# Values as high and low columns with sums on VectorE, and a conv with bf16 taps kept on chip

## The reference

```python
def _L0_cond_ref(x, mask, Wq, Wo):
    xt = jnp.transpose(x, (0, 2, 1))
    q = xt @ Wq.T
    qh = q.reshape(B, T, NH, dk).transpose(0, 2, 1, 3)
    scores = scale * jnp.einsum('bhqd,bhkd->bhqk', qh, qh)
    logits = (scores * cmask + (1.0 - cmask) * NEG) * rmask
    attn = jax.nn.softmax(logits, axis=-1)
    ctx = jnp.einsum('bhqk,bhkd->bhqd', attn, qh)
    out = ctx.transpose(0, 2, 1, 3).reshape(B, T, D) @ Wo.T
    return jnp.transpose(out, (0, 2, 1))

def _L1_cond_ref(x, w, b):
    y = jax.lax.conv_general_dilated(x, w, window_strides=(1,), padding=[(K - 1, 0)], feature_group_count=D, ...)
    return y + b

x = x + _L0_cond_ref(x, cond_2048, L0_cond_Wq, L0_cond_Wo)
x = x + _L1_cond_ref(x, cond_2048[:, None, :], L1_cond_b)
```

## Time and profile before

| | |
|---|---|
| median of three runs | 4569.91 us (4569.88 to 4571.38) |
| profiled execution | 4572.62 us |
| its span in the profile | 4570.9 us |
| mean granted clock | 0.94 of full speed |
| attention, to the last residual | 4068.6 us |
| from there to the first conv matmul | 51.0 us |
| conv from there to the end | 451.3 us |

### The profile page before, as it was taken

The page is one execution under the profiler, slowest core; times in us unless marked ns, Lnnn a source line. Parts: engine busy times, 40 slices in busy tenths (PEclk is TensorE's granted clock), DMA queues, the critical chain, the costliest instruction groups (busy, mean ns, idle before and its releaser), DMA issues. The chain is left out here.

```text
span 4570.9 us, 54681 instructions
## 1 busy us (share of the span) xinstructions
PE 4372.5 (96%) x17536; PEld 3215.0 (70%) x17536; DVE 2754.8 (60%) x2405; ACT 2849.6 (62%) x3777; POOL 2606.2 (57%) x1044
## 2 busy tenths in 40 slices
PE   6999999999999999999999999999999999949999
PEld 4776767676766767676767676676767676729999
DVE  4665646565555556565655555565656565619998
ACT  4776757576766767576767667675757676722332
POOL 3775757575666757575757667575757576620000
PEclk8999999999999999999999999999999999975555
DMA  3324223333323232232333232323323332233442
GB/s 97 79 65 102 66 57 87 74 88 79 91 69 81 66 102 66 69 88 69 86 79 88 70 81 68 97 66 78 82 68 84 79 88 70 60 122 126 148 157 83
DMA packets 205368, 385.70 MB, mean 84 GB/s; under 512 B 17960, under 2 KB 119976, under 8 KB 205096
## 3 DMA queue, kind: packets, MB, share of 16 engines
q1 hardware_dynamic: 205096, 382.08, 32.1%
HBM read 112.79 MB, written 67.11 MB: 39 GB/s over the span
## 5 line engine op out<-in xcount | busy, mean ns | idle before, releaser
L579 POOL TENSOR_TENSOR plo<-p,phi 128x1024 fp32r<-128x1024 f32 x1024 | 2600.5, 2551 | 1422.2 <-ACT phi L529 1411.7
L622 DVE TENSOR_REDUCE mrow<-misc 128x1 f32<-128x1024 f32 x1024 | 1214.9, 1217 | 1082.3 <-PE misc L373 1078.2
L527 ACT ACTIVATE p<-sc 128x512 f32<-128x512 f32 x2048 | 1110.6, 594 | 854.9 <-PE sc L410 605.2
L423 PE MATMUL pv<-phi,val 128*128 128x512 f32 x4096 | 1139.4, 400 | 41.5 <-issue 41.5
L529 ACT ACTIVATE phi<-p 128x1024 fp32r<-128x1024 f32 x1024 | 1086.0, 1061 | 32.5
L423 PEld LDWEIGHTS pv<-phi,val 128*128 128x128 f32 x4096 | 769.1, 189 | 249.4 <-issue 76.1
L409 PE MATMUL sc<-quer,keys 128*128 128x512 f32 x2048 | 919.5, 449 | 24.2 <-issue 18.8
L410 PE MATMUL sc<-quer,keys 96*128 96x512 f32 x2048 | 815.7, 398 | 0.0
L427 PE MATMUL pv<-plo,val 128*128 128x512 f32 x2048 | 648.6, 398 | 0.7 <-POOL plo L579 0.7
L373 PE MATMUL misc<-quer,keys 128*128 128x512 f32 x2048 | 596.5, 399 | 22.7 <-DMA keys<-lo 11.6
L409 PEld LDWEIGHTS sc<-quer,keys 128*128 128x128 f32 x2048 | 387.6, 189 | 202.0 <-issue 76.4
(11 more groups left out here) (49 smaller groups left out, 3319.4 us busy)
## 6 DMA issues: line engine op xcount, KB each, us to landing
keys<-hi SPq DMA_DIRECT2D x256, 256.0 KB, 3.1
quer<-mhi SPq DMA_DIRECT2D x256, 256.0 KB, 4.4
xb<-x SPq DMA_DIRECT2D x16, 2048.0 KB, 8.8
keys<-lo SPq DMA_DIRECT2D x128, 256.0 KB, 4.9
quer<-mlo SPq DMA_DIRECT2D x128, 256.0 KB, 3.8
xo<-x SPq DMA_DIRECT2D x64, 512.0 KB, 4.1
x<-xo SPq DMA_DIRECT2D x64, 512.0 KB, 5.3
xin<-x SPq DMA_DIRECT2D x8, 4096.0 KB, 19.9
```

The costliest lines, as they stand in the source:

```text
L423: pe.matmul(pv[:, half(h)], val[:, i, t, part, :], phi[:, t % NPHI, half(h)], start=(t == 0 and part == 0), stop=False)
L527: act.activation(p32[:, t % NP32, half(h)], sc[:, h, :], ACT.Exp, scale=SCALE).then_inc(s_p32, 1)
L579: pool.tensor_tensor(plo[:, t % NPLO, :], p32[:, t % NP32, :], phi[:, t % NPHI, :].bitcast(F32), ALU.subtract).then_inc(s_plo, 1)
L622: reduced = dve.tensor_reduce(mrow[:, q:q + 1], misc[:, k, :], AX.X, ALU.max)
```

## The change

Attention: `val` becomes one block of 128 columns a step, the 64 high values beside the 64 low ones, and the context takes two matmuls with `phi` and two with `plo` a step where it had four and two. ScalarE copies the two halves of `pv` to `ca` and `cb`, and VectorE adds them before normalising. The denominators come from VectorE: `p32` grows from 2 buffers to 9 slots and keeps a head's eight steps; VectorE sums slots 0 to 4 into slot 5 and then slots 5 to 8 into slot 4, each in two halves of the columns (`partial_sum`). TensorE adds up the partitions with eight fp32 products of 128 columns (`denominator`) into 8 partitions, VectorE takes one reciprocal of 8 x 128, and SyncE takes it to DRAM and back to 64 partitions (`denominators`). The tables are rewritten: `mt` goes from step 5 to 6, `vt` from 6 to 5, outputs move to heads (0,1) and (1,0), the normalisation to step 7 of head 0. `q32` shares `lo`'s memory.

Conv: `toep` for all 128 indices is kept on chip in bf16 and built once, from one DMA of taps laid out on the host; `xin` is cut into three bf16 parts (`first_part`, the upper half of `rest`, `last_part`), all left in the order of `xin`, so that the six matmuls of an index read their weights with a step. The bias comes by one more matmul of 512 columns a bank (`pick` times `brow`), and ScalarE evicts. `x1` is laid out in halves of 64 indices and loaded in halves.

```diff
-MAX_AT = {0: [0, 1], 1: [2, 3], 2: [4], 3: [5], 4: [6, 7]}
-MT_AT = 5
-VT_AT = 6
-REC_AT = {(0, 5): [0], (0, 6): [1], (0, 7): [2], (1, 0): [3], (1, 1): [4], (1, 2): [5], (1, 3): [6], (1, 4): [7]}
-NORM_AT = (1, 5)
+MAX_AT = {0: [0, 1], 1: [2], 2: [3], 3: [4, 5], 4: [6], 5: [7]}
+MT_AT = 6
+VT_AT = 5
+DEN_AT = 3
+SUM_EARLY = {6: ("own", 0, 1)}
+SUM_LATE = {1: ("last", 1, 0), 2: ("last", 1, 1), 5: ("own", 0, 0)}
+NORM_AT = (0, 7)
...
-OUT_AT = {(0, 1, 7): 0, (1, 0, 0): 1, (1, 0, 2): 2, (1, 0, 4): 3,
-          (1, 0, 6): 4, (1, 1, 0): 5, (1, 1, 2): 6, (1, 1, 4): 7}
+OUT_AT = {(0, 1, 2): 0, (0, 1, 4): 1, (0, 1, 6): 2, (0, 1, 7): 3,
+          (1, 0, 0): 4, (1, 0, 2): 5, (1, 0, 4): 6, (1, 0, 6): 7}
...
+            def denominators(b, p, i):
+                g = head(b, p, i)
+                sp.wait_ge(s_rden, g + 1)
+                sp.dma_start(rscr[i].rearrange("(k n) -> k n", n=P), rden8[:, i, :]).then_inc(s_rscr, 16)
+                sp.wait_ge(s_rscr, 16 * g + 16)
+                if i == 0 and not (isinstance(b, int) and pair(b, p) == 0):
+                    sp.wait_ge(s_cnorm, pair(b, p))
+                sp.dma_start(rden[DK * i:DK * i + DK, :],
+                             rscr[i].rearrange("(o t) -> o t", o=1).to_broadcast([DK, T])).then_inc(s_rden_in, 16)
...
+            def denominator(phase, b, step, item, which):
+                out, full = take(phase, b, step, item)
+                pe.wait_ge(s_sum, 4 * (head(*which) + 1))
+                for k in range(KT):
+                    last = pe.matmul(out[0:KT, 0:P], unit[:, k, :], p32[:, TOTAL, tok(k)],
+                                     start=(k == 0), stop=(k == KT - 1))
+                last.then_inc(full, 1)
...
-                    for part in range(2):
-                        pe.matmul(pv[:, half(h)], val[:, i, t, part, :], phi[:, t % NPHI, half(h)],
-                                  start=(t == 0 and part == 0), stop=False)
+                    pe.matmul(pv[:, half(h)], val[:, i, t, :], phi[:, t % NPHI, half(h)], start=(t == 0), stop=False)
...
+                if not first:
+                    act.wait_ge(s_plo, n - KT + 1)
+                    if t == 0:
+                        act.wait_ge(s_sum, 4 * head(b, p, i) - 2)
+                    if t == TOTAL:
+                        k, den = bank(phase, b, (p, i, DEN_AT), ("den",))
+                        act.wait_ge(bank_full[k], den + 1)
...
+            def partial_sum(b, p, i, part, h):
+
+                g = head(b, p, i)
+                tiles = (0, HALF_SUM) if part == 0 else (HALF_SUM, KT + 1)
+                dve.wait_ge(s_p32, 2 * (g * KT + (HALF_SUM - 1 if part == 0 else KT - 1)) + h + 1)
+                dve.wait_ge(s_sum, 4 * g + 2 * part)
+                dve.tensor_reduce(p32[:, TOTAL if part else HALF_SUM, half(h)],
+                                  p32[:, slice(*tiles), half(h)].rearrange("p k n -> p n k"), AX.X, ALU.add).then_inc(s_sum, 1)
...
+                dve.wait_ge(s_cab, head(b, p, 1) + 1)
+                dve.tensor_tensor(ca[:], ca[:], cb[:], ALU.add).then_inc(s_added, 1)
+                dve.wait_ge(s_rden_in, 32 * (j + 1))
+                dve.wait_ge(s_added, j + 1)
+                dve.tensor_tensor(ct[:, p, :], ca[:], rden[:], ALU.mult).then_inc(s_cnorm, 1)
...
-        toep = sb("toep", [P, 2, 2, TC, P], F32R)
-        taps = sb("taps_sb", [P, CH, TG], BF16)
+        toep = sb("toep", [P, 2, TG, P], BF16)
+        taps = sb("taps_sb", [P, 2, TG, CH], BF16)
...
+            def place_taps(h, g):
+
+                for w in range(2):
+                    dve.tensor_scalar(toep[:, w, h * TH:(h + 1) * TH, g * CH:(g + 1) * CH],
+                                      taps[:, w, h * TH:(h + 1) * TH, :], group[:, g:g + 1], None,
+                                      ALU.mult).then_inc(s_toep, 1)
+
+            def parts(k):
+                dve.wait_ge(s_first, k + 1)
+                dve.tensor_tensor(rest[:, k % 2], raw(k), first_part[:, k % 2], ALU.subtract).then_inc(s_rest, 1)
+                dve.wait_ge(s_rest, k + 1)
+                dve.tensor_tensor(last_part[:, k % 2], rest[:, k % 2], upper(rest[:, k % 2]), ALU.subtract).then_inc(s_last, 1)
...
+                slabs = (first_part[:, k % 2], upper(rest[:, k % 2]), last_part[:, k % 2])
...
+                    extra = brow[:, n0:n0 + PER_BANK * NG].unsqueeze(2).to_broadcast([P, PER_BANK * NG, CH])
+                    pe.matmul(acc[at % NBANK][:], pick[:], extra, start=True, stop=False, skip_group_check=True)
...
-                        pe.matmul(o, hi[:, NB:SLOTS], t0, start=True, stop=False)
-                        pe.matmul(o, hi[:, 0:P], t1, start=False, stop=False)
-                        pe.matmul(o, lo[:, NB:SLOTS], t0, start=False, stop=False)
-                        last = pe.matmul(o, lo[:, 0:P], t1, start=False, stop=True)
+                        t0, t1 = toep[:, 0, q * TC + j, :], toep[:, 1, q * TC + j, :]
+                        for slab in slabs:
+                            pe.matmul(o, slab[:, NB:SLOTS, j], t0, start=False, stop=False, skip_group_check=True)
+                            last = pe.matmul(o, slab[:, 0:P, j], t1, start=False, stop=slab is slabs[-1],
+                                             skip_group_check=True)
```

More of the change, by code:

```diff
@@ L48, in misc_items @@
             items.append(("vt",))
+    if t == DEN_AT and not first_head:
+        items.append(("den",))
     if i == 0 and t in PROJ_AT and has_next_pair:
@@ L62, in batch_items @@
                 end = last and p == PAIRS - 1
-                steps[(p, i, t)] = misc_items(p, i, t, first and p == 0, not first, not end, not (end and i == 1))
+                steps[(p, i, t)] = misc_items(p, i, t, first and p == 0 and i == 0, not first, not end, not (end and i == 1))
     return steps
@@ L72 @@
     "last": batch_items(False, True),
-    "end": {"out": [("out", o) for o in range(2 * DT)]},
+    "end": {"den": [("den",)], "out": [("out", o) for o in range(2 * DT)]},
 }
@@ L207, in before, with slot @@
             return (b, p - 1) if p > 0 else (b - 1, PAIRS - 1)
+        def slot(t):
+            return t if t < HALF_SUM else t + 1
         def head_before(b, p, i):
@@ L475, in end @@
                     context(B - 1, PAIRS - 1, 1, t, False)
+                denominator("end", B - 1, "den", ("den",), (B - 1, PAIRS - 1, 1))
                 for item in PHASES["end"]["out"]:
@@ L855, in _ @@
+            first(0)
+            first(1)
             for k in range(ALL):
-                high(k)
+                for f in range(FILLS):
+                    evict(FILLS * k + f)
+                if k + 2 < ALL:
+                    first(k + 2)
         @block.vector
         def _(dve):
+            def place_taps(h, g):
[3 more added lines that the diff above has]
+                                      ALU.mult).then_inc(s_toep, 1)
@@ L893, in _ @@
-            for k in range(2):
-                build_taps(k)
-                low(k)
+            dve.tensor_reduce(tri[:], keep[:].rearrange("p w (g l) -> p w l g", l=CH), AX.X, ALU.max).then_inc(s_own, 1)
+            dve.tensor_reduce(group[:], eye[:].rearrange("p (g l) -> p g l", l=CH), AX.X, ALU.max).then_inc(s_own, 1)
+            dve.wait_ge(s_own, 3)
+            dve.wait_ge(s_taps, 16)
+            own_b = own[:].unsqueeze(1).to_broadcast([P, TG, CH])
+            dve.tensor_tensor(taps_f32, taps_f32, own_b, ALU.add).then_inc(s_own, 1)
@@ L896, in _ @@
+            dve.wait_ge(s_own, 4)
+            for w in range(2):
+                tri_b = tri[:, w:w + 1, :].to_broadcast([P, TG, CH])
+                dve.tensor_tensor(taps[:, w], taps_f32, tri_b, ALU.mult).then_inc(s_own, 1)
+            dve.wait_ge(s_own, 6)
+            for g in range(NG):
+                place_taps(0, g)
+            bias_rows()
             for k in range(ALL):
-                results(k)
-                if k + 2 < ALL:
-                    build_taps(k + 2)
-                    low(k + 2)
+                parts(k)
+                if k < PER_LOAD:
+                    place_taps(1, k)
```

285 lines of the change are left out of this document (154 added, 131 removed).

## The result

The changed kernel takes 6069.37 us (median of four runs, 6067.93 to 6071.14) against 4569.90: a ratio of 1.328 [1.326, 1.331]. 5860 had been predicted. The profiled execution took 6071.14 us, its span is 6069.4, the mean granted clock 0.868.

A forecast was written before the change was run, and what follows sets the result against it. TensorE was taken to bound the old kernel's attention, busy 244.7 of 250.4 us a batch, with VectorE bounding after the change. Attention 5440, conv 421 and 1.7 gave 5863, say 5860 us; range 4950 to 6350.

The forecast's parts named there:

- the wide step's price: VectorE's sums in attention: reads stepping 4096 bytes cost 1.75 ns an element, 134 us a batch.
- The wait at a head's start: Attention: VectorE idles 3.75 us until the row DMA, first scores and maximum finish; low clock adds 1.2 us.
- The waits at the two projections: Attention heads with projections: VectorE waits 4.0 us at the first, 0.8 beyond the sum at the second; 19 a batch.
- The dense price: Rival for attention's sums: 1.04 ns an element despite the step, batch 285 us, total 5030 us; chance 0.16.
- VectorE's work: Attention: VectorE's busy time rises from 143.4 to 264.5 us a batch.
- The waits: Attention: VectorE's idle time, 73 us a batch, added to its 264.5 us of work to give 337.
- 20 + 6 + 19 + 10: Attention waits a batch, us: head starts 20, late maxima 6 and 7 6, projections 19, low clock 10.
- The denominators' term: Attention: VectorE idles 1.1 us a head before the reciprocal, while the denominator's matmuls take 2.0 us; 9 a batch.
- The conv: Conv stage: 421 us against 502, from 42 before the first matmul, 371 for 64 chunks and 8.
- a rival, chance 0.14: Conv faster: bf16 matmuls 0.055 us apart, a chunk 3.1 us, total 5690 us; chance 0.14.
- The lead-in: Conv before its first matmul: tap DMA, VectorE passes, placements and bias rows take 42 us in place of 51.
- The rival of a faster kernel: Attention: removed matmuls count in full, sums hide in TensorE's shadow, batch 235 us, total 4230 us; chance 0.06.

The follow-up runs named there:

- the dense kernel: Changed kernel with each reduce of `p32` grouping neighbouring elements instead of stepping from slot to slot, same element count: 5306.7 us.
- The run with one product less: Kernel before the change without its product of `phi` and the low values, 128 matmuls a batch fewer: 4379.77 us against 4570.93.
- that with short sums: Changed kernel with each of a head's four sums covering 16 of 512 columns: 4415.27 us against 4571.65 for the kernel before.
- The one other placing of the same sums that was tried: Changed kernel with a head's own two sums moved behind `mneg`, to the end of steps 6 and 7: 6056.01 us.
- a third buffer: Old attention with the new conv, `first_part`, `rest` and `last_part` in three buffers instead of two: 4328.22 us, ratio 0.947.

## Why the prediction was right, and where it was off

**The sign and its mechanism were right.** The chain that it named is the one in the trace: the wide step's price, VectorE as the bound, the sums ahead of `mneg`, TensorE idle until the row arrives. The price of 1.75 ns an element gave 3.7 and 4.6 us; measured 3.82 and 4.68, and the dense kernel shows that the step is its cause. The wait at a head's start was 3.75 us plus 1.2 at the low clock, 4.95; measured 4.93 in two heads of the batch, and 6.34 in its first. The waits at the two projections were 4.0 and 0.8 us; where no output projection stands between, 4.3 to 5.0 and 0.83 are measured. TensorE is below 75%, as forecast, but VectorE is busy 71% of a batch, not near 80%. The dense price would have given 5030 us by the prediction; the run with it gave 5307.

**VectorE's work was 8.7 us a batch too high.** The addition and the product of the normalisation were taken at 5.5 us a pair, from the `ct` that runs beside GpSimd; they take 2.45 us, since they now lie in the wait for the row, when GpSimd is idle too: 12 us less. The op was the right one, what runs beside it was not. The other way, the products with `mask` in the staging of a pair (`mhi`, `mlo`) cost 17.3 us a batch where they had cost 15.0, since `mhi` now takes 3.1 us, and the sums 135.2 in place of 134.

**The waits were mis-sized, 102.6 us a batch instead of 73**, and this is where the time of a batch went over. VectorE's idle time of the batch by what ended it: products of maxima 58.8 us, where the prediction has 55 (20 + 6 + 19 + 10); the denominators 20.4, predicted 9; the outputs 17.2, predicted 9; 6 in small gaps. The denominators' term failed because their sixteen instructions were priced at the high clock, 2.0 us; behind a wait they take 2.94 to 3.58. The low clock had been counted at a head's start only, though the prediction had the row for it. Sixteen times the 21 us that remain of both errors make 336 of the 337 by which attention is over.

**The conv was mis-sized the other way, by 129 us.** TensorE does bound it and the clock is up, but the spacing was wrong: 0.111 us had been taken from the float32r products; bf16 goes 0.107 apart already at the low clock and 0.0626 at the high one. A chunk takes 3.94 us, not 5.8. The 0.0626 lies between the two values of the text, 0.055 (a rival, chance 0.14) and 0.111 (the forecast), much nearer to the rival's. The high clock itself was taken over from a row of other products: it came out, but no run shows why the granted clock is 1.00 in this stage and stayed at 0.50 in the one before, where TensorE never waited either. The Trainium skill's 81 ns for a load with its product ("TensorE: Matmul & The Clock Gate", Back-to-back issue gap) is above what this trace shows, 62.6 ns; the trace decides. The lead-in was 31.5 us, not 42: the placements take 0.40 each, the lower end of what was given. Without this error the forecast would have been 5734 us, and the miss 337 us instead of 208 (both against the profiled 6071): 129 of the 337 us are hidden by an error of opposite sign. That part of the closeness is luck.

**The rival of a faster kernel was priced too well.** It let the removed matmuls count in full, 4230 us. The run with one product less shows 191 us for matmuls of 478 (16 x 29.9), and that with short sums shows that the denominators and the order spend even these. The one other placing of the same sums that was tried gives back 13 us; that no better one exists isn't shown.

## What to carry to other kernels

Before work is moved from a full engine to one with idle time, ask how much the full engine can give at all: here 12 of 30 us a batch came back, with nothing put in the place of the removed work. Idle time is worth what the order lets one use: 9 us in one piece on an engine that hands two buffers back and forth stopped its partner in both places tried, and the partner's clock fell with it. And test halves of a double change alone: the conv half wins 210 us, and 242 with a third buffer, which the attention half had buried.

## What the runs showed of the hardware

- A VectorE reduce in SBUF costs 1.04 ns a float32 element between neighbours (2.82 us for 2560) and 1.77 ns with a step of 4096 bytes (4.68 us), each over 0.15 us an instruction. That is near the 1.68 seen at 64 bytes and the 1.83 of a bf16 read at 256: between these steps the penalty doesn't grow.
- TensorE's bf16 loads and products of 128 columns go 0.0555 us apart with dense weights and 0.061 to 0.063 with a step of 16 or 32 bytes, at clock 1.00; the same in float32r were 0.213 apart in a stage where the granted clock stayed at 0.50 though TensorE never waited.
- Two-operand additions on VectorE take 1.22 us for 1024 elements beside an idle GpSimd and 3.44 beside its subtraction, which is longer too, 2.80 us on the mean against 2.38 in the kernel after; one-operand reduces are left alone (one over 2560 elements that runs beside two subtractions, from 2576.34 us in the kernel after, takes 4.53 us, the mean 4.68).
- The conv's granted clock in the kernel after was 0.50 from 5808.9 to 5813 us, behind 32 us of idling, and 1.00 from 5850 to 5950 us.
